# Two images of a convolution and attention kernel joined more closely: scales and first rows earlier, second convolution spread over the head steps, final sum split

## What is computed

```
xn = groupnorm(x)                               # per image and channel
windows of 16 x 16; q, k, v = conv3(xn_w); 64 tokens of 128 features
layernorm of q, k, v; 8 heads; softmax(q k^T + bias) v; projection
xr = xn + attention
y  = xr + conv3(gelu(conv3(xr, c1)), c2) + c2b
out = x + y
```

## Time and profile before

| | us |
|---|---|
| median of 3 runs | 852.24 (850.86 to 852.25) |
| the profiled execution | 853.24 |
| its span on the core | 851.1 |

### The profile page before, as it was taken

The page is one execution under the profiler, slowest core; times in us unless marked ns, Lnnn a source line. Parts: engine busy times, 40 slices in busy tenths (PEclk is TensorE's granted clock), DMA queues, the critical chain, the costliest instruction groups (busy, mean ns, idle before and its releaser), DMA issues.

```text
span 851.1 us, 19126 instructions
## 1 busy us (share of the span) xinstructions
PE 761.1 (89%) x5704; PEld 537.6 (63%) x5704; DVE 660.4 (78%) x2142; ACT 605.7 (71%) x1287; POOL 483.2 (57%) x1041
## 2 busy tenths in 40 slices
PE   0479999999788999999888999999989899999988
PEld 0347777766356777767445777776735677777753
DVE  6558888878657888878675888887866788888575
ACT  1498888765478888876457888877556888886651
POOL 5468677752237777764144776776233677776410
PEclk9999999999999999999999999999999999999999
DMA  7110123000231030300052013110014212000004
GB/s 250 56 29 30 48 108 106 1 1 1 87 125 55 28 128 0 106 1 2 1 166 70 29 30 126 52 55 1 1 56 137 64 34 78 0 1 2 1 1 148
DMA packets 17655, 47.14 MB, mean 55 GB/s; under 512 B 2080, under 2 KB 2720, under 8 KB 17568
## 3 DMA queue, kind: packets, MB, share of 16 engines
q1 hardware_dynamic: 17568, 46.09, 16.6%
HBM read 37.69 MB, written 8.39 MB: 54 GB/s over the span
## 4 chain that ended last, share of the span: by engine, by line
PE 44%; issue 19%; DVE 16%; POOL 11%; ACT 8%; DVEq 1%; DMA 0%; SPq 0%; ACTq 0%; POOLq 0%
PE y_ps L998 12%; PE o_ps L1065 7%; PE pt_ps L1055 5%; PE s_ps L1044 5%; POOL ln_rs L715 4%; PE s_ps L1087 4%; DVE ln_st L540 3%; ACT qk_n L840 3%; PE ox_ps L1014 3%; PE y_ps L969 2%; ACT sc L855 2%; PE t_ps L1023 2%; ACT v_bd L848 2%; DVE h_hi L509 2%; PE y_ps L993 1%
## 5 line engine op out<-in xcount | busy, mean ns | idle before, releaser
L840 ACT ACTIVATE qk_n<-y_ps,ln_nr,ln_rs 128x128 f32<-128x128 f32 x256 | 103.5, 456 | 81.8 <-POOL ln_nr L718 81.1
L998 PE MATMUL y_ps<-w_hi,x_hi 128*128 128x192 f16 (+1 forms) x512 | 149.9, 293 | 0.0
L998 PE MATMUL y_ps<-w_hi,x_lo 128*128 128x192 f16 (+1 forms) x512 | 149.5, 292 | 0.0
L998 PE MATMUL y_ps<-w_lo,x_hi 128*128 128x192 f16 (+1 forms) x512 | 149.5, 292 | 0.0
L728 POOL TENSOR_TENSOR sc<-sc,mx 128x512 f32<-128x512 f32 x128 | 133.7, 1045 | 22.0 <-DVE mx L566 21.5
L1065 PE MATMUL o_ps<-v_bd,pt 128*128 128x66 f32 x1024 | 128.6, 268 | 0.0
L1065 PEld LDWEIGHTS o_ps<-v_bd,pt 128*128 128x128 f32 x1024 | 124.5, 192 | 0.2
L551 DVE TENSOR_TENSOR sc<-s_ps,biasS 128x512 f32<-128x512 f32 x128 | 86.5, 676 | 47.4 <-PE s_ps L1044 45.4
L540 DVE BATCH_NORM_STATS2 ln_st<-y_ps 128x6 f32<-128x128 f32 x384 | 88.7, 286 | 42.6 <-PE y_ps L998 35.5
L715 POOL TENSOR_TENSOR ln_rs<-ln_ve,neg_half 128x3 f32<-128x3 f32 x128 | 113.0, 883 | 10.7
L711 POOL TENSOR_TENSOR ln_ve<-ln_mv,eps_y 128x3 f32<-128x3 f32 x128 | 24.8, 194 | 154.1 <-DVE ln_mv L545 153.8
(11 more groups left out here) (161 smaller groups left out, 1636.5 us busy)
## 6 DMA issues: line engine op xcount, KB each, us to landing
xs<-in_x_sh_dram SPq DMA_DIRECT2D x32, 576.0 KB, 3.9
xst<-in_x_al_dram SPq DMA_DIRECT2D x16, 512.0 KB, 6.8
xf<-in_x_al_dram SPq DMA_DIRECT2D x32, 256.0 KB, 4.2
out_dram<-xf SPq DMA_DIRECT2D x32, 256.0 KB, 2.4
wst<-in_wqkv_dram SPq DMA_DIRECT2D x1, 768.0 KB, 3.8
w1s<-in_w_dram SPq DMA_DIRECT2D x1, 256.0 KB, 8.7
w2s<-in_w_dram SPq DMA_DIRECT2D x1, 256.0 KB, 8.7
biasS<-in_bias_t_dram SPq DMA_DIRECT2D x1, 256.0 KB, 9.4
```

The lines of the kernel that those rows point to most:

```text
L840: ins = act.activation(qk_n[j][:, t, :].rearrange("p (h y x) -> p h y x", h=HEADS, y=2), by_head(y_ps[j][:, E * t:E * (t + 1)]), ACT.Identity,
L998: ins = pe.matmul(y.rearrange("p (t e) -> p t e", t=3)[:, :, cols], xx[r % 2][:, s, a % 2, 2 * TS * (a // 2):2 * TS * (a // 2 + TS)], ww[: ...
```

## The change

It has four parts.

- **Scales and first rows earlier.** The moments of the next image are taken at the end of step 31, the two means in steps 32 and 33 (in a bank of `t_ps`, and PE waits in its queue for DVE), the variance and POOL's power in step 33, the scales in step 34. In step 35, ahead of their other work there, ACT runs the two row passes and the rounding of row 0, and DVE the borders of both rows.
- **c2 spread.** The head is now steps -4 to 3. PE runs c2 tiles 0 and 1 in step -4, behind the first q/k/v group, and one in each of steps -3 to 2. Tiles 2 to 7 use the banks of `pt_ps`, `o_ps` and `ox_ps`, which the new image does not need yet. The last splits and the second border of h are in steps -4 and -3 on DVE.
- **Final sum split.** In steps 20 to 24, 28 and 32 and once after step 35, ACT scales a tile of xr and adds the bias (`scaled`), and POOL adds it to the input tile (`add`). What is left for DVE behind c2 is one pass. Eight input buffers take the place of four, and SP loads all of them at once, behind the loads of rows 4 to 7.
- **start_xr** moves to steps -3 to 0, behind a wait for the last split of the old xr.

```diff
+        c2_bank = [c_ps[3], c_ps[2], pt_bank, o_bank[:, :], ox_ps[:, :], pt_bank, o_bank[:, :], ox_ps[:, :]]
+        c2_in = {-4: (0, 1), -3: (2,), -2: (3,), -1: (4,), 0: (5,), 1: (6,), 2: (7,)}
+        result_in = {-3: (0, 1), -2: (2,), -1: (3,), 0: (4,), 1: (5,), 2: (6,), 3: (7,)}
+        start_in = {-3: 0, -2: 1, -1: 2, 0: 3}
+        sum_in = {20: 0, 21: 1, 22: 2, 23: 3, 24: 4, 28: 5, 32: 6}
...
 # DVE, step
+                if last is not None:
+                    for t in result_in.get(i, ()):
+                        result(last, t)
+                if i == PAIRS + 3 and followed:
+                    for r in range(2):
+                        row(r, (b + 1) * NROW)
...
+                    if i == PAIRS - 1:
+                        moments(b + 1)
                 for t in low_in.get(i, ()):
                     low(b, t)
+                if followed and i == PAIRS:
+                    mean_scale(b + 1)
+                if followed and i == PAIRS + 1:
+                    variance(b + 1)
+                if followed and i == PAIRS + 2:
+                    row_scales(b + 1)
+                    start_scales(b + 1)
+                if last is not None and i == -4:
+                    low(last, 10)
+                    low(last, 11)
+                if last is not None and i == -3:
+                    low(last, 12)
+                    border(last, T1N, 2)
 
             def result(b, t):
                 v.wait_ge(c2_done, b * T2N + (t + 1))
-                v.scalar_tensor_tensor(yt[t % 2][:, :], c2_bank[t], c2_scale[:, 0:1],
-                                       xr[:, T2R * t:T2R * (t + 1), :].rearrange("p i j -> p (i j)"),
-                                       ALU.mult, ALU.add).then_inc(res_added, 1)
-                v.wait_ge(res_added, b * T2N + (t + 1) + RES0)
-                v.wait_ge(xf_biased, b * T2N + (t + 1))
-                v.scalar_tensor_tensor(xf[t % NXF][:, :], yt[t % 2][:, :], x_down[:, 0:1], xf[t % NXF][:, :],
-                                       ALU.mult, ALU.add).then_inc(y_ready, 1)
+                v.wait_ge(xf_summed, b * T2N + (t + 1))
+                v.scalar_tensor_tensor(xf[t][:, :], c2_bank[t], y_down[:, 1:2], xf[t][:, :], ALU.mult,
+                                       ALU.add).then_inc(y_ready, 1)
...
 # POOL
+            def add(b, t):
+
+                if t == 0:
+                    pool.wait_ge(xf_loaded, b * (T2N * 16) + T2N * 16)
+                pool.wait_ge(xd_done, b * T2N + (t + 1))
+                pool.tensor_tensor(xf[t][:, :], xf[t][:, :], xd[t % 2][:, :], ALU.add).then_inc(xf_summed, 1)
...
                 for r in split_in.get(i, ()):
                     split(b, r)
+                if i in sum_in:
+                    add(b, sum_in[i])
+                if followed and i == PAIRS + 1:
+                    inverse(b + 1)
...
 # ACT, step
+                if i == PAIRS + 3 and followed:
+                    act.wait_ge(xn_scales, b + 2)
+                    for r in range(2):
+                        row(r, (b + 1) * NROW, (b + 1) * (NROW // 2))
+                    for z in range(2):
+                        high(0, z, (b + 1) * PAIRS, (b + 1) * NROW)
...
                 for r in split_in.get(i, ()):
                     split(b, r)
+                if i in sum_in:
+                    scaled(b, sum_in[i])
+                if i in start_in:
+                    if last is not None:
+                        act.wait_ge(xr_split, last * NROW + NROW)
+                    act.wait_ge(gn_chain, b * 7 + 7)
+                    start_xr(start_in[i])
+
+            def scaled(b, t):
+
+                act.wait_ge(xr_added, b * NROW + (t + 1) + ADD0)
+                if t >= 2:
+                    act.wait_ge(xf_summed, b * T2N + (t - 1))
+                act.activation(xd[t % 2][:, :], xr[:, T2R * t:T2R * (t + 1), :].rearrange("p i j -> p (i j)"),
+                               ACT.Identity, scale=x_down[:, 0:1], bias=vec[:, C2B:C2B + 1]).then_inc(xd_done, 1)
...
 # PE, step
+                    elif last is not None:
+                        pe.wait_ge(gelu_done, last * T1N + (11 + m))
...
+                if last is not None:
+                    for t in c2_in.get(i, ()):
+                        c2(last, t)
...
+                if followed and i == PAIRS:
+                    pe.wait_ge(qkt_done, h0 + PAIRS // 2)
+                if followed and PAIRS <= i < PAIRS + 2:
+                    mean_of_phases(b + 1, i - PAIRS + 1, gmv[:, 0:1] if i == PAIRS else gm[:, 2:3])
```

More of the change, by code:

```diff
@@ L325, in image @@
                     row(b, r)
+                sp.wait_ge(stored, b * (T2N * 16) + 16)
+                for t in range(T2N):
+                    sp.dma_start(xf[t][:, :], x_al[b, :, 512 * t:512 * (t + 1)]).then_inc(xf_loaded, 16)
                 if followed:
@@ L350, in _ @@
             images(sp, image)
-            for i in range(NXF):
-                sp.wait_ge(stored[i], 16 * B * T2N // NXF + 16)
+            sp.wait_ge(stored, 16 * B * T2N + 16)
         @block.vector
@@ L617, in image @@
                 if followed:
-                    scales(b + 1)
-                    start_scales(b + 1)
-                    row(0, (b + 1) * NROW)
-                    row(1, (b + 1) * NROW)
-                for t in range(BORDER1, T1N):
-                    low(b, t)
-                border(b, T1N, 2)
-                for t in range(T2N - len(HEAD)):
-                    result(b, t)
-                if followed:
-                    head(b + 1, step, result)
-                else:
-                    for t in range(T2N - len(HEAD), T2N):
+                    head(b + 1, step, b)
+                else:
+                    for t in range(BORDER1, T1N):
+                        low(b, t)
+                    border(b, T1N, 2)
+                    for t in range(T2N):
                         result(b, t)
@@ L923, in _ @@
                 act.activation(hi[:, :, :], w[:, :, :], ACT.Identity, scale=w_up[:, j:j + 1]).then_inc(c_hi_done, 1)
-            act.wait_ge(gn_chain, 7)
-            head(0, step, lambda b, t: start_xr(t - 5) if t >= 5 else None)
+            head(0, step)
             images(act, image)
@@ L972, in c1, with by_feature @@
                 ins.then_inc(c1_done, 1)
-            def by_feature(m, p0, r0):
+            def by_feature(m, p0, r0, last=None):
                 if has(m):
                     pe.wait_ge(normed, p0 + (m + 1))
+                    if m == 0 and last is not None:
+                        pe.wait_ge(y_ready, last * T2N + T2N + 1)
                     if m % 4 == 0:
@@ L1034, in step @@
                     pe.wait_ge(qkt_done, h0 + (h + 1))
-                    if i == 0:
-                        pe.wait_ge(res_added, b * T2N + RES0)
+                    if i == 0 and last is not None:
+                        pe.wait_ge(y_ready, last * T2N + 2 + 1)
                     if i >= 1:
@@ L1051, in step @@
                     pe.wait_ge(exped, p0 + (m + 1))
+                    if m == 0 and last is not None:
+                        pe.wait_ge(y_ready, last * T2N + 6 + 1)
                     if m >= 1:
@@ L1061, in step @@
                     pe.wait_ge(pt_copied, p0 + (m + 1))
+                    if m == 0 and last is not None:
+                        pe.wait_ge(y_ready, last * T2N + 7 + 1)
                     if m >= 1:
```

169 lines of the change are left out of this document (68 added, 101 removed).

## The result

| | before | after |
|---|---|---|
| median | 852.25 us (850.86 to 852.36) | 876.24 us (874.33 to 878.31) |
| the profiled execution | 853.24 | 874.33 |
| its span | 851.1 | 872.5 |

The ratio is 1.029, interval 1.025 to 1.032: slower, by 24 us. The sign was forecast, the size was not: 856.3 was predicted and the range ended at 862.

What follows compares the result with a forecast made beforehand. PE was taken to set the pace in the body and bound the transition. Profiled 853.2 + 26.8 (spread sums) + 0.0 (small parts) - 22.7 (transitions) = 857.3 us, 856.3 in the median's terms; range 845 to 862.

Steps and rivals of the forecast that it cites:

- The body: Steps 20 to 32 of each image: the spread sums were to cost 6.7 us per image, 26.8 for four.
- the loop: Steps 20 to 24: exp, scaled copy, POOL's sum and scale chain wait in turn; five exp intervals take 27.7 us, not 21.7.
- The image's end: Ahead of the new image: PE idle 2.2 us before second mean and 3.5 before c1 11; first convolution ends 4.65 later.
- The clock: After PE's idle at each transition: one stretch at the lower clock, 0 to 1.7 us, taken as 1.7.
- rival D: Each transition: a second stretch at the lower clock after the 2.2 us idle, +5.1 us, 861.4 us; chance 0.14.
- PE's sum: New image's first q/k/v group to scores of step 3: PE is the bound all through, 40.0 us.
- rival E: Head steps: tiles do not spread but run in a row as before, most gain lost, about 870 us; chance 0.04.
- the sum of 69.3: Scores of step 31 to step 3 of the next image: 69.3 us per transition, the three saving 22.7 us.
- small parts: Last image's end, input loads, and moving start_xr and the weight split in the first head: each put at 0 us.
- B: Body: sums half hidden since POOL finds the scaled copy ready, 13.4 us instead of 26.8, 843 us; chance 0.15.
- C: Image's end: mean comes earlier and clock stays up, 2.2 and 0.9 us less per transition, 847 us; chance 0.23.
- A: Whole kernel, the forecast itself: sums cost as the split does, PE bounds the transition, 856.3 us (853.9 to 860); chance 0.44.

## Why the prediction was right and wrong

- **The body, right in mechanism, mis-sized in its term.** Exps at 5.7 us with POOL waiting for ACT before each sum were named as the sign that the loop is right, and they are there. The term of 6.7 us per image is 7.9. The exps of steps 20 to 25 gave 28.84 - 21.69 = 7.15 instead of 6.0. The loop was copied from the split's 5.39, with 1.05 us for the sum from POOL's subtraction and, as the other bound, 1.12 from the split. The sum takes 1.27 (1266 to 1356 ns over 32), outside my bounds, and the scaled copy 0.82, where I had put it 0.1 above the rounding's 0.64. With the true durations the split's loop gives the measured one: 5.39 + (1.27 - 1.12) + (0.82 - 0.64) = 5.72 us against 5.71. That is nearly all of the 4.9 us. The fifth interval, with the ot copies, came out at 5.98 (forecast 6.05) by luck: it stays at 5.99 with the sum one step later, so no such loop sets it. Step 28 cost what was left, 0.75 against 0.7.
- **The image's end, right in the first transition.** Second mean: 13.9 us after the scores of step 31, idle 2.44 (forecast 13.8 and 2.2). Tile c1 11: 223.06 - 199.01 = 24.05 us after them, idle 3.48 (forecast 24.06 and 3.5). The 0.8 us allowed for the sum beside the splits is seen as passes of 1.25 and 1.44 us where 0.38 and 0.56 are plain, 1.75 in all, part of which before had too. In the second and third transitions tile c1 11 comes 25.0 and 25.6 us after the scores, since PE is at the lower clock from the second mean on.
- **The clock, under-sized.** One stretch of 3.4 us at 1.2 GHz was forecast per transition. The first had 6.8 us in one piece, the second two stretches of 3.4, the third one. So rival D, a second stretch, came in two of three. The first group of the new image came 30.0 us after the scores instead of 29.3.
- **PE's sum, right.** From that group to the scores of step 3: 268.86 - 229.04 = 39.8 us against 40.0. The tiles do spread; rival E is out. PE is busy for all of these 39.8 us. That the 4.3 us in the sum, an estimate, fit so well is partly luck. The transition is 69.8, 70.0 and 70.6 against 69.3.
- **The failed step: the jump.** The 77.95 and 77.32 us of before held the jump of the images' loop, the 75.30 did not; the sum of 69.3 replaced all three alike, and so took the jump out. It only moved behind the window, where "small parts" had nothing, and cost 4.7 us each time: 9.7 with the 0.3 of the third. The jump was put at nothing; written out, the two kernels give back 9.5 and 7.3 us. It is the largest part of the 17.0 us that are missing, and no term of the sum stood for it. The hint was in the earlier trace rows: three transitions with the same work, one of them 2.0 to 2.7 us shorter. Which copy of the code a step is in belongs to what a change moves, and I had not asked.
- **The rivals.** B (sums half hidden, 843) is out: no interval came under 4.9. C (cheaper end, 847) is out. The bounds of A do not come out of its own terms: 0.9 us less for each of three transitions gives 853.6, not 853.9, and 0.07 more for each of 32 sums 858.5, not 860. The side slower was right; the range missed the time by 14 us because it took in no case for the jump and no bound for the sum above the nearest rows.

## What to carry over

Where two engines work in order, ask of each added pair of operations whether the second waits for the first inside one step while a chain that the first needs next is queued behind it; one step later the same work cost 6 us instead of 31. A shorter stretch between two marks is no saving until it is known that what left it has not moved past the mark: copies of the same stretch that differ, as 75.3 beside 78.0, name what is in it. An operation moved to make room on one queue must be followed to who waits next for that queue: the rows moved late freed PE 3.8 us sooner and lost 12 us.

## What the runs showed of the hardware

- The jump back of a long loop, whose body is a whole image, leaves DVE idle for 4.3 and 4.4 us and ACT for 3.9 and 4.0 with nothing to wait for, and PE for 2.2 and 2.6. At the first jump of the change 3.3 us at 1.2 GHz follow, at the second none, and both cost the same. Written out, the change gains 9.5 us and before 7.3, for two jumps.
- POOL's sum of two whole f32 operands of 128x512 takes 1.27 us; its subtraction of the same shape, whose second operand is a maximum per head and token spread over 64 places, takes 1.04.
- Idles of the same length on PE came with different stretches at 1.2 GHz. In before an idle of 2.2 us is followed by 3.4 us of it in all three transitions. In the change the idle of 2.4 us is followed by 3.4 us of it in the second and third transition and by none in the first; the idle before tile c1 11 comes with 6.8 us in the first (3.5 us idle), 3.4 in the second (3.0 idle) and none in the third (3.5 idle). Written out, all three idles of 3.4 us come with 6.8 us of it.
